# Reordering the second stage of a decoder kernel: feed-forward output behind the last values, quantisation tile by tile, layer rows transposed ahead of the values

## What is computed

```python
x = _layernorm(x + _L0_attn_ref(x, ...))            # first stage; its last norm is in the second
x = _layernorm(x + _L0_xattn_ref(x, ctx_1024, mask_BxS2_bk1, Wq, Wkv, Wo, bo))
x = _layernorm(x + _L0_ffn_ref(x, w_gate, w_up, w_down))

# cross attention, 16 heads of 64, over 256 context tokens
sim = clip(where(mask, q @ k.T * SCALE, max_neg), -5.0, 5.0)
out = softmax(sim) @ v;  out = out @ Wo + bo

# feed-forward with quantised activations and ternary weights
_act_quant(x): scale = 127 / max(|x|, axis=-1);  round(x * scale) / scale
gate = silu(_bitlinear(x, w_gate));  up = _bitlinear(x, w_up)
return _bitlinear(gate * up, w_down)
```

## Time and profile before

| what | us |
|---|---|
| median of 3 runs (lowest, highest) | 4131.1 (4127.99, 4131.69) |
| the profiled execution | 4129.27 |
| its span, first to last instruction | 4127.5 |

### The profile page before, as it was taken

How to read it: one execution, slowest core, us unless ns; L and a number is a source line. 1 busy time by engine, 2 the same in 40 slices (tenths; PEclk the granted TensorE clock), 3 DMA queues, 4 the chain that set the end, 5 groups by cost and what they waited for, 6 DMA issues and landing times. The chain is left out here.

```text
span 4127.5 us, 168644 instructions
## 1 busy us (share of the span) xinstructions
PE 3926.8 (95%) x70234; PEld 2224.9 (54%) x70266; DVE 3645.2 (88%) x10777; ACT 3179.3 (77%) x6589; POOL 2061.5 (50%) x2326
## 2 busy tenths in 40 slices
PE   6999999999999999999999993999999999999997
PEld 3555555555555555555555552666666666666664
DVE  8999999999999999999999996778888878888886
ACT  4999999999999999999999993566666666656664
POOL 3666666666666666666666663333333333333332
PEclk9999999999999999999999997999999999999998
DMA  2000000000000000000000002000000100000100
GB/s 76 23 22 22 22 21 22 22 23 22 22 22 23 22 22 21 23 22 22 22 22 22 22 23 104 19 22 22 22 22 22 32 22 22 22 22 22 32 14 9
DMA packets 98260, 105.18 MB, mean 25 GB/s; under 512 B 17200, under 2 KB 95696, under 8 KB 96360
## 3 DMA queue, kind: packets, MB, share of 16 engines
q1 hardware_dynamic: 97496, 94.39, 7.8%
HBM read 48.68 MB, written 17.69 MB: 16 GB/s over the span
## 5 line engine op out<-in xcount | busy, mean ns | idle before, releaser
L550 POOL TENSOR_TENSOR conv_products<-normed_features,conv_taps_by_token 128x256 f32<-128x256 f32 (+1 forms) x852 | 781.2, 917 | 609.3 <-DVE convolved_features L503 358.2
L749 POOL TENSOR_TENSOR exps_of_both_halves<-scores 128x256 f32<-128x256 f32 x512 | 401.1, 805 | 735.9 <-ACT scores L961 735.9
L263 PE MATMUL banks<-up_centred,after_cell_features 128*32 128x336 f32 x9088 | 759.6, 452 | 0.0
L961 ACT ACTIVATE scores<-scores 128x512 f32<-128x512 f32 x512 | 305.4, 626 | 170.8 <-DVE scores L1084 170.8
L239 PE MATMUL banks<-down,hidden_features 112*32 112x256 f32 x6816 | 427.3, 383 | 0.0
L319 ACT ACT_TABLE_LOAD x284 | 364.4, 1283 | 52.3 <-PE banks L219 47.3
L1084 DVE SCALAR_TENSOR_TENSOR scores<-banks,score_top 128x512 f32<-128x512 f32 x512 | 327.5, 680 | 83.3 <-PE banks L808 83.3
L540 POOL TENSOR_TENSOR conv_partial_sums<-conv_products,conv_partial_sums 128x512 f32<-128x512 f32 x284 | 364.8, 1285 | 66.1 <-DVEq L439 43.9
L263 PEld LDWEIGHTS banks<-up_centred,after_cell_features 128*32 128x32 f32 x9088 | 237.2, 109 | 270.6 <-issue 270.6
L340 ACT ACT_TABLE_LOAD x284 | 364.4, 1283 | 5.0
L212 PE MATMUL banks<-recurrent_weights,h_features 64*32 64x256 f32 x9088 | 311.7, 383 | 1.4 <-ACT h_features L312 1.4
(11 more groups left out here) (204 smaller groups left out, 9718.2 us busy)
## 6 DMA issues: line engine op xcount, KB each, us to landing
layer_inputs<-layer_outputs SPq DMA_DIRECT2D x284, 96.0 KB, 2.0
layer_inputs<-in_x SPq DMA_DIRECT2D x285, 32.0 KB, 1.7
x_scratch<-layer_outputs SPq DMA_DIRECT2D x284, 32.0 KB, 1.8
layers_out<-x_scratch SPq DMA_DIRECT2D x32, 256.0 KB, 2.9
x_tokens<-in_x SPq DMA_DIRECT2D x32, 256.0 KB, 3.1
context_features<-in_ctx SPq DMA_DIRECT2D x32, 256.0 KB, 3.8
out<-result SPq DMA_DIRECT2D x64, 128.0 KB, 1.9
up_centred<-in_ff_up SPq DMA_DIRECT2D x1, 2688.0 KB
```

What stands on the lines that cost most here:

```text
L263: mm = nc.tensor.matmul(bank[group(l), b, 0:UP], xmt[:, n, group(l)], up[:, l, n, at:at + UP], start=n == 0, stop=n == HALF - 1, skip_grou ...
L550: nc.gpsimd.tensor_tensor(prod[:, i:i + n], xnt[:, j % NRING].rearrange("p n t -> p (n t)")[:, None, :].broadcast_to([P, n, HALF * P]), ta ...
L749: nc.gpsimd.tensor_tensor(psum[:, i % RING, :], pr[:, i % RING, 0:S], pr[:, i % RING, S:2 * S], ALU.add).then_inc(halves_added, 1)
L961: nc.scalar.activation(pr[:, i % RING, :], pr[:, i % RING, :], ACT.Exp, scale=S_SCALE).then_inc(exp_done, 1)
```

## The change

Five edits, all in the second stage. No arithmetic, buffer or DMA is changed.

- `transpose_x` takes one tile; tile 0 stands ahead of unit 5, tile 1 behind it, and `feed_in(f, 0)` behind that with its old count in a new spelling. ACT's `x_features` is split in the same way around `unit_hi` of unit 5.
- `x1_features(j + 1)` moves from behind quad 0's values to ahead of them.
- `feed_out(f)` moves from inside quad 3 to behind its second half of values.
- `round_up` and `round_down` of both tiles become `quantised(tt)`, up and down of one tile. For x, tile 0 is ahead of and tile 1 behind `unit_lo(j, 2)`; for the hidden values tile 0 is at s_ = 3, tile 1 at s_ = 4. `x_quantised` gives the semaphore count of a tile in the new order.
- On DVE the second moments and the second norm of x1 move behind the last `attended` of the batch.

```diff
+    def x_quantised(j, tt):
+        return QUANT * j + QUANT - 2 * (QT - 1 - tt)
...
@@ tensor
-            def transpose_x(j):
-                for tt in range(QT):
-                    pe.wait_ge(quant_step, QUANT * j + QUANT - QT + tt + 1)
...
+            def transpose_x(j, tt):
+                pe.wait_ge(quant_step, x_quantised(j, tt))
...
                 if r == 0:
-                    pe.wait_ge(xqt_done, QT * (j + 1))
+                    pe.wait_ge(xqt_done, QT * j + QT)
...
                 if j > 0:
-                    transpose_x(f)
-                for r in range(ROUNDS):
+                    transpose_x(f, 0)
+                unit(j, UBANKS)
+                if j > 0:
+                    transpose_x(f, 1)
+                    feed_in(f, 0)
+                for r in range(1, ROUNDS):
                     unit(j, UBANKS + r)
                     if j > 0:
                         feed_in(f, r)
...
                     if q + 1 < QUADS:
                         scores(j, 2 * q + 2)
+                    if q == 0 and j + 1 < B:
+                        x1_features(j + 1)
                     attend(j, q, 0)
-                    if q == 3 and j > 0:
-                        feed_out(f)
                     if q + 1 < QUADS:
                         scores(j, 2 * q + 3)
                     denominators(j, q)
                     attend(j, q, 1)
-                    if q == 0 and j + 1 < B:
-                        x1_features(j + 1)
                     if q == 2 and j > 0:
                         transpose_h(f)
+                    if q == 3 and j > 0:
+                        feed_out(f)
                     if q > 0:
                         out_project(j, 2 * q - 2)
                         out_project(j, 2 * q - 1)
@@ scalar
                 if j > 0:
-                    x_features(f)
-                for r in range(ROUNDS):
+                    x_features(f, [0])
+                unit_hi(j, UBANKS)
+                if j > 0:
+                    x_features(f, [1])
+                    silu(f, 0)
+                for r in range(1, ROUNDS):
@@ vector
+            def quantised(j, tt, src, rounded, dst, step):
                 dve.wait_ge(step, QUANT * j + QT + 2)
+                nc.vector.tensor_scalar(rounded[:, tt, :], src[:, tt, :], q127[:, tt:tt + 1], ROUND, ALU.mult, ALU.add).then_inc(step, 1)
+                dve.wait_ge(step, x_quantised(j, tt) - 1)
+                nc.vector.tensor_scalar(dst[:, tt, :], rounded[:, tt, :], -ROUND, 127.0, ALU.add, ALU.min).then_inc(step, 1)
...
                     scales(f, quant_step, 0, 2)
-                    round_up(f, x2, xqf, quant_step)
-                    round_down(f, xqf, xq, quant_step)
+                    quantised(f, 0, x2, xqf, xq, quant_step)
                 unit_lo(j, 2)
+                if j > 0:
+                    quantised(f, 1, x2, xqf, xq, quant_step)
...
-                        elif s_ == 3:
-                            round_up(f, hf, gate, hquant_step)
-                        elif s_ == 4:
-                            round_down(f, gate, hq, hquant_step)
-                    if later:
-                        if s_ == 5:
-                            x1_moments(later, 0)
-                            x1_first_norm(later)
-                            x1_moments(later, 1)
-                        if s_ == 6:
-                            x1_second_norm(later)
+                        elif s_ < 5:
+                            quantised(f, s_ - 3, hf, gate, hq, hquant_step)
+                    if later and s_ == 5:
+                        x1_moments(later, 0)
+                        x1_first_norm(later)
                 attended(j, QUADS - 1)
+                if later:
+                    x1_moments(later, 1)
+                if later:
+                    x1_second_norm(later)
```

More of the change, by code:

```diff
@@ L864, in out_project @@
                     mm.then_inc(att_ready, 1)
-            def transpose_x(j):
-                for tt in range(QT):
-                    pe.wait_ge(quant_step, QUANT * j + QUANT - QT + tt + 1)
[L869 to L874, removed]
+            def transpose_x(j, tt):
+                pe.wait_ge(quant_step, x_quantised(j, tt))
+                if j > 0:
+                    pe.wait_ge(z_done, QT * (j - 1) + tt + 1)
+                for h in range(HALF):
+                    mm = nc.tensor.transpose(bank[:, FFB + tt, :].bitcast(BF16)[:, h * P:(h + 1) * P],
+                                             xq[:, tt, h * P:(h + 1) * P], identb[:])
+                mm.then_inc(xqt_ready, 1)
             def feed_in(j, r):
@@ L950, in _ @@
             f = B - 1
-            transpose_x(f)
+            for tt in range(QT):
+                transpose_x(f, tt)
             for r in range(ROUNDS):
@@ L967, in rstds, with x_features @@
                 nc.scalar.activation(dst[:], log[:], ACT.Exp, scale=-0.5).then_inc(step, 1)
-            def x_features(j):
-                for tt in range(QT):
+            def x_features(j, tiles):
+                for tt in tiles:
                     act.wait_ge(xqt_ready, QT * j + tt + 1)
@@ L1062, in _ @@
                         h_features(f)
-                    if q == 3 and later:
-                        x1_rstd(later, 1)
+                if later:
+                    x1_rstd(later, 1)
                 if j > 0:
@@ L1069, in _ @@
             nc.scalar.preload_act_table(ACT.Silu)
-            x_features(f)
+            x_features(f, range(QT))
             for r in range(ROUNDS):
@@ L1112, in scales @@
                                         qstep[:, :, None].broadcast_to([P, QT, c1 - c0]), ALU.mult).then_inc(step, 1)
-            def round_up(j, src, rounded, step):
+            def quantised(j, tt, src, rounded, dst, step):
                 dve.wait_ge(step, QUANT * j + QT + 2)
[L1116 to L1122, removed]
+                nc.vector.tensor_scalar(rounded[:, tt, :], src[:, tt, :], q127[:, tt:tt + 1], ROUND, ALU.mult, ALU.add).then_inc(step, 1)
+                dve.wait_ge(step, x_quantised(j, tt) - 1)
+                nc.vector.tensor_scalar(dst[:, tt, :], rounded[:, tt, :], -ROUND, 127.0, ALU.add, ALU.min).then_inc(step, 1)
             def x_abs_max(j):
@@ L1313, in _ @@
             scales(f, quant_step, 0, 2)
-            round_up(f, x2, xqf, quant_step)
-            round_down(f, xqf, xq, quant_step)
+            for tt in range(QT):
+                quantised(f, tt, x2, xqf, xq, quant_step)
             for r in range(ROUNDS):
@@ L1320, in _ @@
             scales(f, hquant_step, 2, 3)
-            round_up(f, hf, gate, hquant_step)
-            round_down(f, gate, hq, hquant_step)
+            for tt in range(QT):
+                quantised(f, tt, hf, gate, hq, hquant_step)
             fed(f)
```

3 lines of the change are left out of this document (2 added, 1 removed).

## The result

| | before | with the change |
|---|---|---|
| median of 6 runs (lowest, highest), us | 4130.58 (4127.99, 4131.95) | 4161.44 (4159.05, 4163.45) |
| ratio, with its 95% interval | | 1.0076 (1.0066 to 1.0086) |
| span of the profiled execution, us | 4127.5 | 4159.3 |

What follows compares the result with a forecast made beforehand. The prediction took PE to bound the second stage, every pause of it paid in full. Terms of +34.7, +7.5, 0 and 0 gave +42.2 us on the profiled 4129.3, so 4171 us, range 4149 to 4189.

Steps and rivals of the forecast that it cites:

- Part 1: First feed-forward matmul: waits for tile 1's copy, no longer covered by unit 5; 1.12 us PE idle a batch, +34.7 us.
- The claim that nothing is bought back: Behind the first feed-forward matmul: all later work shifts by the same 1.12 us, DVE and ACT get no work ahead.
- Part 2: Attention phase, f32 transposes ahead of values: 0.27 us won at L818, but 0.25 a batch lost overall, +7.5 us.
- ring: Attention phase: later denominators delay ACT's log and exponential, DVE's `attended`, then clips for scores 5 and 7, by 0.25 us.
- Part 3: DVE rounding of x and hidden values tile by tile: same instructions in another order, 0 us.
- signs of being wrong: No idle at first feed-forward matmul, score waits much below 31 us, or hidden roundings' mean moving over 0.2 us.
- for x: 0: Rounding of x: tile 1 ready one `unit_lo` later, but PE comes for it a whole unit later; 0 us.
- Part 4: Quad 3 and batch end: feed-forward output behind last values, x1's second norm behind `attended`; no instruction added, 0 us.
- The gain of part 2 is kept: Rival, chance 0.15: the 0.27 us a batch at L818, behind the v eviction, stays won; 4155 us.
- Rounding meets POOL badly: Rival, chance 0.1: DVE queue between clips 10 and 14, one more rounding behind a POOL add, 0.47 a batch; 4186 us.
- Faster: Rival, chance 0.05: PE comes late enough that both score waits and the v-eviction wait vanish, -14 us; 4115 us.
- no change: Rival, chance 0.05: the attention phase's waits go and just pay for the pause at the feed-forward matmul; 4127 us.

Runs made afterwards that it cites:

- e1: Kernel before with only the transpose of x tile 1, and its copy on ACT, moved behind unit 5: 4163.1 us, ratio 1.0079.
- e3: Kernel before with only the f32 transposes of the next batch's rows moved ahead of quad 0's values: 4139.5 us, ratio 1.0022.
- e6: Changed kernel with both x transposes and copies ahead of unit 5 again, and x's rounding in the old order: 4127.9 us, ratio 0.9996.
- e4: Kernel before with only the feed-forward output moved from between the last quad's value halves to behind them: 4120.4 us, ratio 0.9977.
- e5: Changed kernel with ACT's copy of x tile 1 ahead of unit 5's eviction instead of behind it: 4151.4 us, ratio 1.0052.
- e2: Changed kernel with both x transposes and copies ahead of unit 5 again, new rounding order kept: 4154.5 us, ratio 1.0054.
- e8: Kernel before with feed-forward output behind the last values and DVE's queue reordered so clips freeing banks of scores 5 and 7 come first: 4091.1 us, ratio 0.9905.
- e7: Kernel before with the feed-forward output between the denominators and second values of quad 3: 4128.8 us, ratio 0.9999.

## Why the prediction was right, and where it was off

| part | forecast, us | measured alone, us | by rows, us a batch |
|---|---|---|---|
| 1, split around unit 5 | +34.7 | +32.6 (e1) | +1.02, forecast 1.12 |
| 2, f32 transposes earlier | +7.5 | +9.1 (e3) | +0.31 at scores 7, forecast 0.25 |
| 3, rounding by tiles | 0 | not alone; -0.5 left with the norm's move (e6) | 0 |
| 4, output behind the values | 0 | -10.1 (e4) | -0.32, forecast 0 |
| sum | +42.2 | 31.6 | +1.01 |

The parts measured alone add up to 31.6 us, and the change is 30.9. The sum was 11 us too high, and 10.1 of that is part 4. That parts 1 and 2 together are so near, 41.7 measured against 42.2, is in part luck: one was 2.1 high, the other 1.6 low.

**Part 1** was right in its mechanism: the wait for both copies, unit 5 as its cover, the eviction ahead of the copy in ACT's queue. e5 shows the last by itself. The step that was mis-sized is the last one, "the load stands at 3343.33 where it stood at 3342.20", 1.12 us of PE idle (these figures give 1.13). The weight load does come 1.11 us later (3359.46, on the old scale 3343.31; here 16.15 are to be taken off). But from the load to the first matmul of the records are 0.23 us now and were 0.32 (3342.20 to 3342.52): the old load ran ahead under the matmuls of unit 5, and that lead was not PE's to lose. By unit 6, the next row behind it, 1.02 are lost. **The claim that nothing is bought back** held: from unit 6 to scores 2 the two kernels go in step within 0.02.

**Part 2** was right, ring and all, and a little low. Of the shift of 0.32 I let 0.07 be absorbed at `attended`; nothing was. The shift arrived whole, which had been the upper bound. In both kernels `attended` starts 0.10 behind the end of ACT's exponential (3312.23 and 3312.33; on the old scale 3312.55 and 3312.65), where I had put 0.03. So ACT already reached it as late as the clips did, and nothing was left to absorb the shift.

**Part 3** came out at 0 as argued: the down starts 0.03 us behind the end of its up (3336.09, 3336.12), and the way to clip 12 is not longer. That the roundings and POOL's adds are both longer where they meet agrees with the blocking that the prediction names. One of its signs of being wrong came up all the same, a mean of the hidden roundings that moves by over 0.2 us: in the stage the ups went from 1028 to 791 ns. It was a bad sign, for the downs took over what the ups gave up. And "for x: 0" had the condition that PE comes for tile 1 a whole unit later. e2 shows what the condition is worth: 24 us without it.

**Part 4** is the step that failed: "Neither adds an instruction", and so "0 us". I counted instructions and waits and not what stands beside what. `feed_out` stood between narrow matmuls, with a pause on each side, and now stands beside the full-width projections. The list of weight-load pauses in the profile before had these places, with counts of 96, 127 and 65 by line. Their price in PE's time shows only beside the rows after: 0.12 more for the values in front of `feed_out` (1.00) than in front of the denominators (0.88), 0.10 for `feed_out` and 0.09 for the projections.

**The rivals.** "The gain of part 2 is kept" falls by e3. "Rounding meets POOL badly" falls by the unchanged busy time, 117.5 us. "Faster" and "no change" supposed that the score waits shrink: they grew from 31.0 to 35.5.

## What to carry to other kernels

A transpose, its copy out of PSUM and the matmul that reads it need other PE work between the first and the last. Without it PE waited 0.70 us here with ACT free (e5), and 1.08 with an eviction ahead in ACT's queue. Half a split is worth nothing while the wait behind it counts both tiles. By the code that wait could itself be split: round 0's gate matmuls read tile 0 and write bank 6, and only its up matmuls write bank 7, where tile 1's transposes lie. That kernel was not run.

Price edits of a chain together. The late rounding of tile 1 without the late transpose costs 24 us (e2), the late transpose alone 33 (e1), and the change with both 31 and not 57: the transpose is so late that the rounding is done by then.

On a PE that is busy 97% of a stage, the order of matmul shapes (10 us, e4) and the order of DVE's queue ahead of the clips that free PE's banks (28 us, e8 less e4) were worth more than the wait that part 2 went after (0.27 us a batch, 8 us).

## What the runs showed that I had not expected

In quad 3, going from matmuls on a 32-column weight tile to ones on a full-width tile or back costs PE about 0.16 us at each change, an estimate from e4: -0.33 us a batch for two changes fewer. With their number unchanged it was 0.00 (e7). In these changes the weight load is not taken ahead. The last projections' first load starts 0.01 us ahead of its matmul behind the values (3330.66 and 3330.67), and 0.11 ahead of it behind `feed_out` (3328.05 and 3328.16, e4). The load shows a pause without a partner of 0.2 to 0.4 us (26.8 us in 127 times at L830, 26.8 in 65 at L861). Such pauses are not at these changes alone (42.9 us in 127 times at the score matmuls, whose tiles have 64 rows), and e8 has a change without one. Why the load does not go ahead there was not tried.
